# Expert weight slabs moved to other parts of a shared buffer, first loads issued earlier, in an attention plus mixture-of-experts layer on eight cores

## The reference

```python
x = layernorm(x + attention(x))        # 16 heads of 128, rotary, softmax, output projection Wo
# mixture of experts, E = 8 experts, hidden size 1024; all experts are computed for all tokens
rw   = sigmoid(x @ Wg.T)               # two largest kept and normalised to sum 1 -> expert_w
h1   = einsum('th,efh->tef', x, W1)
h3   = einsum('th,efh->tef', x, W3)
g    = silu(h1) * h3 * expert_w[:, :, None]
out  = einsum('tef,ehf->th', g, W2)
x = layernorm(x + out)
```

## Time and profile before

| | us |
|---|---|
| median of 3 runs | 3528.25 |
| lowest and highest run | 3486.62, 3878.09 |
| profiled execution, device time | 3488.89 |
| its span on the slowest core (core 2) | 3487.2 |
| spans of the eight cores | 3480.0 to 3487.2 |
| TensorE busy on core 2 | 2737.5 (79%) |
| VectorE, ScalarE, GpSimd busy | 908.2, 709.8, 163.8 |
| mean granted TensorE clock, all cores | 0.886 to 0.889 |

### The profile page before, as it was taken

The page is one execution under the profiler, slowest core; times in us unless marked ns, Lnnn a source line. Parts: engine busy times, 40 slices in busy tenths (PEclk is TensorE's granted clock), DMA queues, the critical chain, the costliest instruction groups (busy, mean ns, idle before and its releaser), DMA issues.

```text
span 3487.2 us, 32955 instructions; the slowest of 8 cores (3480.0 to 3487.2 us)
## 1 busy us (share of the span) xinstructions
PE 2737.5 (79%) x12081; PEld 1238.5 (36%) x12290; DVE 908.2 (26%) x1439; ACT 709.8 (20%) x1113; POOL 163.8 (5%) x308
## 2 busy tenths in 40 slices
PE   1777786877777777867773799999998989898992
PEld 1424242423324242422220344444343434343430
DVE  0222223132232323233116322221212131313125
ACT  0332323333333333343110000000000000000003
POOL 0000000000000000000000000000101010101000
PEclk9878797888878787887885899999999999999996
DMA  9010100100010101000221243444344434444422
GB/s 158 13 24 13 25 13 16 21 12 13 13 25 13 24 13 25 7 7 8 42 36 30 43 76 64 76 64 79 61 79 61 77 63 77 63 74 65 73 43 96
DMA packets 50494, 155.39 MB, mean 45 GB/s; under 512 B 5922, under 2 KB 6050, under 8 KB 49058
## 3 DMA queue, kind: packets, MB, share of 16 engines
q0 software_dynamic: 47024, 142.69, 24.7%
q1 hardware_dynamic: 3314, 10.59, 0.8%
HBM read 287.54 MB, written 8.39 MB: 85 GB/s over the span
## 4 chain that ended last, share of the span: by engine, by line
PE 70%; DVE 11%; DMA 7%; issue 6%; ACT 4%; another core or an unknown queue 1%; DVEq 0%; ACTq 0%; SPq 0%; POOLq 0%
PE pa L720 13%; PE pa L740 13%; PE pa L770 8%; PE pa L268 7%; DMA wslab<-w_t 6%; PE pa L343 6%; PE pa L337 5%; PE pa L415 4%; PE pa L495 4%; PE pa L402 4%; PE pa L421 4%; DVE rinv L449 3%; DVE vbuf L569 1%; PE pa L323 1%
## 5 line engine op out<-in xcount | busy, mean ns | idle before, releaser
L770 PE MATMUL pa<-aog,wslab 128*128 128x512 bf16 x2007 | 456.4, 380 | 66.4 <-DMA wslab<-w_t 64.1
L720 PE MATMUL pa<-xy,wslab 128*128 128x512 bf16 x2003 | 466.0, 389 | 3.5 <-issue 1.4
L740 PE MATMUL pa<-xy,wslab 128*128 128x512 bf16 x2009 | 450.4, 379 | 2.1
L409 ACT ACTIVATE scr_bf<-pa,mq_sb 128x512 bf16<-128x512 f32 x512 | 333.4, 686 | 77.5 <-PE pa L402 74.8
L734 ACT ACTIVATE scr_bf<-pa 128x512 bf16<-128x512 f32 x128 | 69.5, 594 | 1303.1 <-PE pa L720 1303.1
L343 PE MATMUL pa<-R_bf,wslab 128*128 128x512 bf16 x768 | 319.0, 415 | 2.1
L770 PEld LDWEIGHTS pa<-aog,wslab 128*128 128x128 bf16 x2048 | 194.3, 98 | 327.4 <-issue 110.5
L337 PE MATMUL pa<-R_bf,wslab 128*128 128x512 bf16 x728 | 305.2, 419 | 0.0
L720 PEld LDWEIGHTS pa<-xy,wslab 128*128 128x128 bf16 x2048 | 203.5, 100 | 255.0 <-issue 24.8
L740 PEld LDWEIGHTS pa<-xy,wslab 128*128 128x128 bf16 x2048 | 200.4, 98 | 241.6
L752 DVE TENSOR_TENSOR scr_bf<-pa,scr_f 128x512 bf16<-128x512 f32 x128 | 88.0, 688 | 751.3 <-PE pa L740 751.3
(11 more groups left out here) (114 smaller groups left out, 1526.6 us busy)
## 6 DMA issues: line engine op xcount, KB each, us to landing
wslab<-w_t POOLq DMA_DIRECT2D x128, 512.0 KB, 5.2
wslab<-w_t POOLq DMA_DIRECT2D x128, 256.0 KB, 3.8
R_bf<-x_t POOLq DMA_DIRECT2D x1, 8192.0 KB, 59.0
wslab<-wv_t POOLq DMA_DIRECT2D x8, 1024.0 KB, 8.4
wslab<-wq_t POOLq DMA_DIRECT2D x8, 1024.0 KB, 8.8
wslab<-wk_t POOLq DMA_DIRECT2D x8, 1024.0 KB, 8.8
wslab<-wo_t POOLq DMA_DIRECT2D x16, 512.0 KB, 5.0
y<-R_f SPq DMA_DIRECT2D x16, 512.0 KB, 2.6
```

Of the source, the lines that this page charges most:

```text
L409: return s.activation(scr_bf.ap()[:, slot * 512:(slot + 1) * 512], pa[bank].ap(), AF.Exp, bias=mq_sb.ap()[:, 6:7], scale=SCALE)
L720: last = t.matmul(pa[nc2].ap(), wslab.ap()[:, W1OFF[s1] + dc * 128: W1OFF[s1] + dc * 128 + 128], xy.ap()[:, dc * TL + nc2 * 512: dc * TL + ...
L740: last = t.matmul(pa[4 + nc2].ap(), wslab.ap()[:, W3OFF[s1] + dc * 128: W3OFF[s1] + dc * 128 + 128], xy.ap()[:, dc * TL + nc2 * 512: dc * ...
L770: last = t.matmul(pa[wb + nc2].ap(), wslab.ap()[:, W2OFF[s2] + fc * 128: W2OFF[s2] + fc * 128 + 128], aog.ap()[:, fc * TL + nc2 * 512: fc ...
```

## The change

Three things change. The definitions of the slabs and of the two pump functions move from behind the router to before the Wo stage, and the two first W1/W3 pairs, `pump_w13(2)`, are recorded there, ahead of the loads of the Wo stage. The slabs of W1 move to columns 4096 to 8191 (keys ws2, ws3), those of W3 to 8192 to 12287 (ws4, ws5), and those of W2 to 0 to 2047. The two W2 slabs, which had a key each ("ws4a", "ws4b"), now have one key between them, "ws0". `pump_w2(2)` stays where it was.

```diff
+    W1OFF = [4096, 6144]
+    W3OFF = [8192, 10240]
+    W2OFF = [0, 1024]
+    W1KEY = ["ws2", "ws3"]
+    W3KEY = ["ws4", "ws5"]
+    W2KEY = ["ws0", "ws0"]
...
+    def pump_w13(n=1):          # moved, text unchanged
+    def pump_w2(n=1):           # moved, text unchanged
...
+    pump_w13(2)
+
     for ec in range(NHC):       # the Wo stage
         sl = ec % 2
         wok = f"ws{sl}"
...
-    W1OFF = [0, 2048]
-    W3OFF = [4096, 6144]
-    W2OFF = [8192, 9216]
-    W1KEY = ["ws0", "ws1"]
-    W3KEY = ["ws2", "ws3"]
-    W2KEY = ["ws4a", "ws4b"]
...
-    pump_w13(2)
     pump_w2(2)
     for e in range(NE):
         emit_h13(e, hook=lambda e=e: emit_ew_rows(e))
         emit_w2(e)
```

More of the change, by code:

```diff
@@ L483, in build_program @@
           r=[f"ao{h}" for h in range(NH)], dma="dbg6")
+    W1OFF = [4096, 6144]
[4 more added lines that the diff above has]
+    W2KEY = ["ws0", "ws0"]
+    w13_q = [(e, fc) for e in range(NE) for fc in range(NFC)]
+    w2_q = [(e, hc) for e in range(NE) for hc in range(NHC)]
+    w13_pos = [0]
+    w2_pos = [0]
+    def pump_w13(n=1):
+        for _ in range(n):
+            if w13_pos[0] >= len(w13_q):
+                return
+            e, fc = w13_q[w13_pos[0]]
+            w13_pos[0] += 1
+            s1 = fc % 2
+            G(lambda g, e=e, fc=fc, s1=s1: g.dma_start(
+                wslab.ap()[:, W1OFF[s1]:W1OFF[s1] + 2048].rearrange(
+                    "p (dc f) -> p dc f", dc=NDC), d_w1[e, fc]),
+                w=[W1KEY[s1]], dma=f"sw1_{s1}")
+            G(lambda g, e=e, fc=fc, s1=s1: g.dma_start(
+                wslab.ap()[:, W3OFF[s1]:W3OFF[s1] + 2048].rearrange(
+                    "p (dc f) -> p dc f", dc=NDC), d_w3[e, fc]),
+                w=[W3KEY[s1]], dma=f"sw3_{s1}")
+    def pump_w2(n=1):
+        for _ in range(n):
+            if w2_pos[0] >= len(w2_q):
+                return
+            e, hc = w2_q[w2_pos[0]]
+            w2_pos[0] += 1
+            s2 = hc % 2
+            G(lambda g, e=e, hc=hc, s2=s2: g.dma_start(
+                wslab.ap()[:, W2OFF[s2]:W2OFF[s2] + 1024].rearrange(
+                    "p (fc h) -> p fc h", fc=NFC), d_w2[e, hc]),
+                w=[W2KEY[s2]], dma=f"sw2_{s2}")
+    pump_w13(2)
     for ec in range(NHC):
```

## The result

| | us |
|---|---|
| kernel before, median of 10 runs | 3487.32 |
| changed kernel, median of 8 runs (lowest) | 4230.48 (4217.14) |
| ratio, with 95% interval | 1.2112 (1.2083 to 1.2141) |
| span of the slowest core, before and after | 3487.2 and 4215.4 |
| mean granted TensorE clock, before and after | 0.886 to 0.889 and 0.814 to 0.842 |

The change makes the kernel 21% slower, 728 us of span. The forecast was 4212 us, in a range of 4145 to 4320; the profiled execution took 4217.1. Some executions of either kernel have one die at a lower clock and are longer; the medians above include them, ratios and readings leave them out, and where too few others are left for a ratio (e3, e6, e7) the lowest run is given, without an interval.

What follows compares the result with a forecast made beforehand. TensorE was taken to bound the expert stages. W2 stages: 119 x (8.1 + 2.1) + 9 x 3.45 = 1244.9 us against 521.4, +723 on 3488.9, so 4212 us; other stages 0; range 4145 to 4320.

Steps and rivals of the forecast that it cites:

- Early loads: First W1/W3 loads, recorded before the Wo stage: gain 0, at most the 0.33 us idle ahead of the first W1 matmul.
- What they are put in front of: GpSimd's queue ahead of the Wo loads: cost 0, with 30 us of cover left before the Wo matmuls start.
- 119 waits: W2 blocks that wait for the next block's load: 7 x 15 + 14 = 119; nine blocks run free.
- 8.1 us for a block at full clock: Each waiting W2 block, start to start: 16 matmuls, then the exposed load, 8.1 us; a free block 3.45 us.
- 2.1 us for the clock: Time lost to TensorE's lowered clock at each W2 wait: chosen 2.1 us, between 0 and 3.4.
- the Wo row: Wo stage before the change: 1.7 us lost to the lower clock at each idle, used as basis for the W2 price.
- The clock holds: Rival for the W2 stages: only the load is exposed, clock stays up; +474, 3962 us; chance 0.08.
- Every burst at half clock: Rival for the W2 stages: all 16 matmuls of each burst at 1.2 GHz; +878, 4367 us; chance 0.08.
- The new wait is free: Rival at the W2 matmuls: each block waits for its own slab alone, not slower, 3489 us; chance 0.04.
- A load alone lands at another speed: Rival on the W2 load's landing: each 0.1 us is 12 us in the sum; no more than 3.9 us expected.

Runs made afterwards that it cites:

- e3: Changed kernel with 16 extra unused matmuls behind each of the 119 W2 blocks after which TensorE waits; lowest of five runs 3964.1 us.
- e6: Changed kernel with four W2 slabs, a key each, and the four summing matmuls of a Wo block moved behind the next block's matmuls; lowest of four runs 3320.5 us.
- e7: Changed kernel with 12 extra unused matmuls behind each W2 block that waits; lower of two runs 3959.5 us.
- e1: Changed kernel with a key for each W2 slab again, new columns and earlier loads kept; ratio to the kernel before 1.0013.
- e2: Kernel before with only the key changed: both W2 slabs, in their old columns, share one key; ratio to the kernel before 1.2078.

## Why the prediction was right, point by point

*Early loads.* Cost and gain 0: right. The first W1 matmul starts at 1905.04, before at 1906.07; e1 as a whole is at 1.0013.

*What they are put in front of.* Cost 0: right. The timeline of GpSimd in the changed kernel has the second pair at 1578 and the first two Wo loads right behind:

```profile
1578.06 0.53 POOL L503 DMA_DIRECT2D wslab<-w_t  x1 [83.35 <-PE pa L290]
1578.58 0.54 POOL L507 DMA_DIRECT2D wslab<-w_t  x1
1579.10 1.08 POOL L529 DMA_DIRECT2D wslab<-wo_t  x2
```

The Wo matmuls start at 1628.2, before at 1628.9.

*119 waits.* Right to the number, in the changed kernel and in e2.

*8.1 us for a block at full clock.* Right: 7.96 us in the rows of e3. The recorded wait of 4.44 us plus 0.17 is 4.61, forecast 4.65.

*2.1 us for the clock.* It was a choice between 0 and 3.4; the trace of the slowest core gives 2.2 (261 / 119). That it fell so near is partly luck: the Wo row alone, 1.7, would have been 0.5 us short at each wait, and nothing in the rows of before fixed how much to add. A block was forecast at 10.2 us and takes about 10.3; the W2 stages were forecast at 1244.9 us and take 1252.5. The reason that I gave for going above 1.7 (a somewhat longer idle, a shorter dense stretch) fits but isn't shown; what the rows do show is in the stretches of two turns of the changed kernel:

```profile
2066.40:2071.00 4.60, 4.60 (x12) 1.52 (x13) 0.00 (x0) 0.00 (x0) 0.00 (x0) 0.50 0.00 0
2071.10:2074.40 3.30, 1.15 (x6) 0.30 (x4) 1.38 (x2) 0.00 (x0) 0.53 (x1) 1.00 0.11 13
2074.50:2077.80 3.30, 1.01 (x3) 0.43 (x4) 0.00 (x0) 0.00 (x0) 0.00 (x0) 0.50 0.37 66
2077.90:2081.20 3.30, 3.30 (x9) 1.18 (x8) 0.00 (x0) 0.00 (x0) 0.00 (x0) 0.50 0.00 0
```

The clock is back at 1.00 only late in the burst, spends that time mostly idle, and has fallen again before the next burst begins. Of the 16 matmuls some two thirds (261 us / 0.211 us = 1240 of 1904) run at the low level; in the Wo stage it was 3.3 us of 9.5. The Trainium skill, TensorE: Matmul & The Clock Gate, section "HAM oscillation — how this bites in real kernels", has each burst behind the wait for a load start throttled. The trace agrees (clock 0.50 at the start of both bursts, 2066.40 and 2077.90 in the rows); but the throttled part ends within the burst, so the 4367 us that the prediction drew from a whole burst at 0.50 are not reached. The Wo rows agree less well than the prediction says: there the first 1.1 us behind the idle is at 1.00 and the 0.50 comes only then.

*The rivals.* "The clock holds" had its mechanism priced rightly, 3962 us, and e3 and e7 reach that time (3964.1, 3959.5) when the idle is filled. "Every burst at half clock" is refuted by the stretch at 1.00. "The new wait is free" is refuted by the 119 waits; e1 shows what it would have been. "A load alone lands at another speed": 3.7 us in the changed kernel, 3.8 before, by the prediction's price worth 12 us at most. That price (12 us for each 0.1 us) does not hold in the changed kernel. The loads of core 3 of the changed kernel land in 4.2 us in the median, and the rows of its L773 matmuls are

```profile
L773 PE MATMUL pa<-aog,wslab x2048: 376/491/634, 2058.0 to 4126.6; 128*128 128x512 bf16 x187
  DMA wslab<-w_t: 579.9, 119
```

It waits 51 us longer than core 5, yet its span is 4215.1 us beside 4215.4: its median matmul is 491 ns in place of 631. On core 0, with loads of 3.5 us, the waits are 510.1 us and the span is 4213.8. A longer wait was paid back by fewer slow matmuls, and the turn stayed at 10.2 us. So the wait and the clock are not two independent terms, as the sum has them; 549 and 261 us is the division on core 5, and on core 3 it is about 600 and 210.

## What to carry to other kernels

Where waits are made from names, a name is a claim on memory: two disjoint buffers under one name are one buffer, and if the refill of the next is recorded ahead of the use of the present one, double buffering turns into load, wait, compute. Price such a loop from the chain of waits at the place where it is already closed (here 8.1 us from free slab to next use), count the waits from the recorded order, and then ask what the idle does to TensorE's clock: here that was a third of the loss (261 of 731 us). Before a deeper rearrangement, look for short waits that repeat; two more slabs gave 2%, four matmuls moved by one block nearly 3%.

## What the runs showed of the hardware that was not expected

Filling the gap does not help in proportion: no run lies halfway. With 12 or 16 extra matmuls (idles mostly of 1.7 and 0.9 us) the clock stays at 1.00 in nearly all blocks (110 of the 119 bursts on the slowest core with 12 are fast) and a block takes about 8.0 us; with 8, 4 or none (3.4, 3.8 and 4.4 us on the slowest core) it falls in most blocks, and a block takes 9.9 to 10.3. The length of one idle does not decide alone: with 4 extra matmuls, neighbouring idles of 3.73 and 3.79 us are followed by a burst at full speed and by a slow one, and with 12 one of 2.52 us by a slow one. What else decides was not tested. In that regime extra work on TensorE can cost nothing or even gain: 1904 additional matmuls made the kernel 253 us faster.

Loads of 256 KB landed in 3.5 to 3.8 us (medians of the cores) on most cores in most kernels, but in 3.9 to 4.5 us with 8 extra matmuls and in 3.9 to 4.0 with 4. Nothing in these runs shows why.
